# Eight one-hot buffers instead of four in the counting sweeps of a four-layer graph kernel

## The reference, cut to what matters

```
bias = bias.at[dst, src].set(edge_weight)          # layer 0: the last edge of a cell wins
agg = segment_sum(h[src] * norm, dst)              # layer 1
msg = h_all[src, edge_type]; agg = segment_sum(msg, dst)   # layer 2
```

## Time and profile before

| what | value |
|---|---|
| median of 3 runs | 592.63 us (592.21 to 593.97) |
| the profiled execution | 597.42 us |
| its span in the profile | 595.7 us |
| PE busy | 533.4 us, 90% of the span |
| DVE busy | 397.4 us, 67% |
| POOL busy | 280.2 us, 47% |
| ACT busy | 226.2 us, 38% |
| mean granted TensorE clock | 0.96 of full speed |

### The profile page before, as it was taken

One profiled execution on the slowest core, in us unless ns is written; L12 is line 12 of the kernel. 1 busy time (PEld: TensorE's weight loads), 2 busy tenths in 40 slices (PEclk: granted clock), 3 DMA queues, 4 the chain that ended last, 5 costly groups with the idle time before them and its releaser, 6 DMA issues.

```text
span 595.7 us, 7620 instructions
## 1 busy us (share of the span) xinstructions
PE 533.4 (90%) x2437; PEld 351.2 (59%) x2452; DVE 397.4 (67%) x939; ACT 226.2 (38%) x473; POOL 280.2 (47%) x271
## 2 busy tenths in 40 slices
PE   6999999978999999888999999959798997999690
PEld 2444444436865546656778888838576885555460
DVE  7987978889757778965658734572246527773736
ACT  3020610035237754573512332333424127774333
POOL 7566556567468775305514300456541735754000
PEclk8999999997999999998999999979999899999896
DMA  7940000000673100236526200156752751100001
GB/s 267 395 108 2 0 0 0 0 1 2 238 226 102 54 19 1 72 109 209 149 67 208 72 0 1 42 170 167 205 158 87 210 154 45 37 1 1 1 0 71
DMA packets 29913, 54.37 MB, mean 91 GB/s; under 512 B 4962, under 2 KB 6446, under 8 KB 29368
## 3 DMA queue, kind: packets, MB, share of 16 engines
q1 hardware_dynamic: 15964, 27.14, 14.8%
q0 software_dynamic: 11968, 19.96, 11.0%
q10 hardware_dynamic: 1948, 6.86, 3.2%
HBM read 51.78 MB, written 2.17 MB: 91 GB/s over the span
## 4 chain that ended last, share of the span: by engine, by line
PE 62%; DVE 16%; ACT 7%; POOL 6%; DMA 6%; issue 3%; ACTq 0%; DVEq 0%; POOLq 0%
PE bank L499 19%; PE bank L476 9%; PE bank L478 9%; PE bank L477 9%; DMA wh<-w 4%; PE bank L594 4%; POOL wl L346 4%; PE bank L578 3%; PE bank L569 3%; ACT gap L769 2%; PE bank L671 2%; DVE h L1044 2%; DVE h L1043 2%; PE bank L669 2%; PE bank L670 2%
## 5 line engine op out<-in xcount | busy, mean ns | idle before, releaser
L346 POOL TENSOR_TENSOR wl<-wraw,wh 128x512 fp32r<-128x512 f32 (+1 forms) x78 | 103.9, 1351 | 86.3 <-DMA wh<-w 21.0
L499 PE MATMUL bank<-hot 128*128 128x512 bf16 x529 | 118.6, 383 | 3.7 <-DVE hot L1092 2.9
L387 POOL DMA_INDIRECT edge_bias<-ewn,cell_at x68 | 75.0, 1103 | 43.7 <-DVE cell_at L1086 19.5
L499 PEld LDWEIGHTS bank<-hot 128*128 128x128 bf16 x544 | 53.5, 99 | 68.5 <-DVE hot L1092 3.4
L476 PE MATMUL bank<-wh,tl 128*128 128x512 f32 x176 | 71.4, 406 | 2.3 <-DVE tl L1003 2.3
L478 PE MATMUL bank<-wh,th 128*128 128x512 f32 x176 | 69.4, 394 | 0.0
L477 PE MATMUL bank<-wl,th 128*128 128x512 f32 x176 | 69.2, 393 | 0.0
L476 PE MATMUL bank<-th,wl 128*128 128x512 f32 x104 | 43.3, 417 | 10.0 <-DVE packed L1179 6.4
L477 PE MATMUL bank<-tl,wh 128*128 128x512 f32 x104 | 42.7, 410 | 0.0
L478 PE MATMUL bank<-th,wh 128*128 128x512 f32 x104 | 42.5, 409 | 0.0
L1091 DVE TENSOR_SCALAR hot<-iota,ef 128x512 bf16<-128x512 f16 x68 | 30.6, 450 | 16.1 <-PE bank L499 8.2
(11 more groups left out here) (188 smaller groups left out, 1023.6 us busy)
## 6 DMA issues: line engine op xcount, KB each, us to landing
wraw<-w SPq DMA_DIRECT2D x26, 256.0 KB
wh<-w POOLq DMA_DIRECT2D x6, 1024.0 KB, 6.2
keyb<-edge_keys ACTq DMA_DIRECT2D x4, 1088.0 KB, 11.1
wh<-w_rel POOLq DMA_DIRECT2D x4, 1024.0 KB, 5.8
wraw<-w_rel SPq DMA_DIRECT2D x16, 256.0 KB
wraw<-w_qkv SPq DMA_DIRECT2D x8, 256.0 KB
wraw<-w_o SPq DMA_DIRECT2D x8, 256.0 KB
wh<-w_o POOLq DMA_DIRECT2D x2, 1024.0 KB, 5.8
```

The costliest lines, as they stand in the source:

```text
L346: pool.tensor_tensor(wl[n % WSLOTS][:, k, 0:width], wraw[:, q % 3, 0:width], wh[n % WSLOTS][:, k, 0:width], ALU.subtract).then_inc(s["w_lo ...
L387: pool.indirect_dma_start(out=bias_dram, out_offset=bass.IndirectOffsetOnAxis(ap=cell_at[:, c:c + 1], axis=0), in_=ewn[:, c:c + 1], in_off ...
L499: mm = pe.matmul(ps(name)[:], hot[:, slot, 0, i * P:(i + 1) * P], hot[:, slot, 1 + kind, :], start=False, stop=last, skip_group_check=True)
```

## The change

Four more buffers, `hot_late`, are laid over the memory of `wl[1]` and `wl[2]`, so that `RING` is 8. DVE may then build eight chunks before PE has used the first of them. The sweeps are counted in chunks (`SWEEPS` = 32 and 36), and PE's loops and DVE's loop of the first sweep run over eight chunks. On DVE, the first four chunks of the second sweep are all built before banks 4 to 7 are copied (three before), its first group needs no wait on `hot_used2`, then a loop runs three times over two groups, and a last group stands alone. The lag of placing is eight chunks as before. Since `wl[1]` and `wl[2]` are now also one-hot buffers, DVE waits ahead of L1173, and POOL ahead of `low(2)`, until PE has used 32 chunks of the second sweep.

```diff
@@ -37,10 +37,9 @@
-RING = 4
-TBLOCKS = CHUNKS // RING
-CBLOCKS = (8, 9)
-FIRST_PLACED = 2
+RING = 8
+SWEEPS = (32, 36)
+BEHIND = 2 * GROUP
...
@@ -49,9 +48,9 @@
-assert E == CHUNKS * P and sum(CBLOCKS) == TBLOCKS and max(CBLOCKS) * RING * P <= 2 * MIDDLE < BASE
+assert E == CHUNKS * P and sum(SWEEPS) == CHUNKS and max(SWEEPS) * P <= 2 * MIDDLE < BASE
-assert RING == GROUP and CBLOCKS[1] == 9
+assert RING == 2 * GROUP == BEHIND and SWEEPS[0] % RING == 0 and SWEEPS[1] % RING == GROUP
 
 
 WEIGHTS = ([("w0_q", K, D), ("w0_k", K, D), ("w0_v", K, D), ("w0_o", K, D), ("w0_1", K, D), ("w1", K, D), ("w2_self", K, D)]
@@ -183,7 +182,8 @@
         deg = sb("deg", [P, 6, T], F32)
         ones = sb("ones", [P, P], F32R)
         wh = [sb(f"wh{s}", [P, K, D], F32R) for s in range(WSLOTS)]
-        wl = [sb(f"wl{s}", [P, K, D], F32R) for s in range(WSLOTS)]
+        lows = region([("hot_late", [P, RING // 2, 3, N], BF16)], [(f"wl{s}", [P, K, D], F32R) for s in range(1, WSLOTS)])
+        wl = [sb("wl0", [P, K, D], F32R)] + [lows[f"wl{s}"] for s in range(1, WSLOTS)]
         wraw = sb("wraw", [P, 3, D], F32)
         nbias = sb("nbias", [P, T, N], F32)
         xh = region([("keyb", [P, E + (WINDOW - 1) * P], F32)],
@@ -205,7 +205,7 @@
...
-        cc = region([("hot", [P, RING, 3, N], BF16), ("packed", [P, 8, N], F32), ("later", [P, WINDOW * P], F16), ("eq", [P, GROUP, WINDOW * P], F16)],
+        cc = region([("hot", [P, RING // 2, 3, N], BF16), ("packed", [P, 8, N], F32), ("later", [P, WINDOW * P], F16), ("eq", [P, GROUP, WINDOW * P], F16)],
...
@@ -217,6 +217,7 @@
         sp = [ab["sp"][:, n, :] for n in range(4)] + [rel_rows, deg_rows]
         rowh1, rowl1, rel_add, counth, countl = (ab[k] for k in ("rowh1", "rowl1", "rel_add", "counth", "countl"))
         hot, packed, call, call2, cph, cpl = (cc[k] for k in ("hot", "packed", "call", "call2", "cph", "cpl"))
+        hot = [hot[:, n] for n in range(RING // 2)] + [lows["hot_late"][:, n] for n in range(RING // 2)]
         later, eq = cc["later"], cc["eq"]
         ei, er, row_key = ab["ei"], ab["er"], ab["row_key"]
         msgh, msgl, hidh, hidl, probT = (cc[k] for k in ("msgh", "msgl", "hidh", "hidl", "probT"))
@@ -390,6 +391,7 @@
             for k in range(WINDOW):
                 pool.wait_ge(scattered[k], 16 * len(range(k, CHUNKS, WINDOW)))
             pool.dma_start(nbias[:], by_tile(bias_dram)).then_inc(s["bias_loaded"], 16)
+            pool.wait_ge(s["hot_used2"], SWEEPS[1] - GROUP)
             low(2)
             cast(3)
             low(3)
@@ -496,25 +498,25 @@
                 pe.wait_ge(s["hot_ready"], total_c)
                 for n, name in enumerate(names):
                     i, kind = n % T, n // T
-                    mm = pe.matmul(ps(name)[:], hot[:, slot, 0, i * P:(i + 1) * P], hot[:, slot, 1 + kind, :],
+                    mm = pe.matmul(ps(name)[:], hot[slot][:, 0, i * P:(i + 1) * P], hot[slot][:, 1 + kind, :],
                                    start=False, stop=last, skip_group_check=True)
                     if last:
                         finish(mm, name)
                 if not last:
                     mm.then_inc(s[f"hot_used{sweep}"], 1)
 
-            def sweep(w, blocks, before, names):
+            def sweep(w, count, before, names):
                 for name in names:
                     begin(name)
                     pe.matmul(ps(name)[:], minus[:], offset[:], start=True, stop=False, skip_group_check=True)
                 for slot in range(RING):
                     chunk(slot, before + slot + 1, w, slot, names, False)
-                with pe.Fori(1, blocks - 1) as b:
+                whole_rings = (count - 1) // RING
+                with pe.Fori(1, whole_rings) as b:
                     for slot in range(RING):
                         chunk(None, b * RING + (before + slot + 1), w, slot, names, False)
-                for slot in range(RING):
-                    c = (blocks - 1) * RING + slot
-                    chunk(c, before + c + 1, w, slot, names, slot == RING - 1)
+                for c in range(whole_rings * RING, count):
+                    chunk(c, before + c + 1, w, c % RING, names, c == count - 1)
 
             def columns(name, w, ready, ks=K, n=K):
 
@@ -600,8 +602,8 @@
             pe.wait_ge(s["centre_set"], 3)
             before = 0
             for c in range(2):
-                sweep(1 + c, CBLOCKS[c], before, [("counts", c, b) for b in range(8)])
-                before += CBLOCKS[c] * RING
+                sweep(1 + c, SWEEPS[c], before, [("counts", c, b) for b in range(8)])
+                before += SWEEPS[c]
             columns("q0", 0, lambda i: pe.wait_ge(s["x_low"], K))
             columns("k0", 1, lambda i: pe.wait_ge(s["k_low"], K))
             rows("v0", 2, lambda i: None)
@@ -1088,23 +1090,24 @@
 
             def build_chunk(j, slot):
 
-                dve.tensor_scalar(hot[:, slot, 0, :], iota[:, 0:N], ef[:, 0, bass.ds(j, 1)], None, ALU.is_equal)
-                dve.tensor_scalar(hot[:, slot, 1:3, :].rearrange("p a n -> p (a n)"), iota[:], pair_dst[:, bass.ds(j, 1)],
+                dve.tensor_scalar(hot[slot][:, 0, :], iota[:, 0:N], ef[:, 0, bass.ds(j, 1)], None, ALU.is_equal)
+                dve.tensor_scalar(hot[slot][:, 1:3, :].rearrange("p a n -> p (a n)"), iota[:], pair_dst[:, bass.ds(j, 1)],
                                   digit[:, bass.ds(j, 1)], ALU.is_equal, ALU.mult).then_inc(s["hot_ready"], 1)
 
-            def build_and_place(sweep, at, first, c, group):
-
-                for slot in range(RING - 1):
-                    dve.wait_ge(s[f"hot_used{sweep}"], at + (slot - RING + 1))
-                    build_chunk(at + (first + slot), slot)
-                    mark(c, slot)
-                mark(c, RING - 1)
-                dve.wait_ge(s[f"hot_used{sweep}"], at)
-                build_chunk(at + (first + RING - 1), RING - 1)
+            def build_and_place(sweep, at, first, slots, c, group):
+
+                for n in range(GROUP):
+                    if n == GROUP - 1:
+                        mark(c, n)
+                    if sweep:
+                        dve.wait_ge(s[f"hot_used{sweep}"], at + (n - RING + 1))
+                    build_chunk(at + (first + n), slots + n)
+                    if n < GROUP - 1:
+                        mark(c, n)
                 settle(c, group)
 
             dve.wait_ge(s["ld_iota"], 16)
-            for slot in range(RING):
+            for slot in range(GROUP):
                 build_chunk(slot, slot)
             for n, value in enumerate((EPS, ROUND, -ROUND)):
                 link(dve.memset(const[:, n:n + 1], value))
@@ -1113,27 +1116,25 @@
             link(dve.memset(keyb[:, E:], -1.0))
             dve.wait_ge(s["ld_ew"], 16)
             link(dve.tensor_scalar(ewn[:], ew[:], 8.0, None, ALU.mult))
-            for block in range(1, FIRST_PLACED):
-                for slot in range(RING):
-                    j = block * RING + slot
-                    dve.wait_ge(s["hot_used1"], j - RING + 1)
-                    build_chunk(j, slot)
+            for slot in range(GROUP, RING):
+                build_chunk(slot, slot)
             dve.wait_ge(s["ld_later"], 16)
             dve.wait_ge(ld_keys[0], 16)
             dve.wait_ge(ld_keys[1], 16)
-            with dve.Fori(FIRST_PLACED, CBLOCKS[0]) as b:
-                build_and_place(1, b * RING, 0, b * RING + (-FIRST_PLACED * RING), b + (-FIRST_PLACED))
-
-            before, behind = CBLOCKS[0] * RING, (CBLOCKS[0] - FIRST_PLACED) * RING
+            with dve.Fori(1, SWEEPS[0] // RING) as b:
+                for half in range(2):
+                    at = b * RING + half * GROUP
+                    build_and_place(1, at, 0, half * GROUP, at + (-BEHIND), b * 2 + (half - BEHIND // GROUP))
+
+            before, behind = SWEEPS[0], SWEEPS[0] - BEHIND
             dve.wait_ge(ld_keys[2], 16)
             dve.wait_ge(ld_keys[3], 16)
-            for slot in range(RING - 1):
+            for slot in range(GROUP):
                 dve.wait_ge(s["hot_used1"], before - RING + slot + 1)
                 build_chunk(before + slot, slot)
             for i in range(T):
                 wait_full(dve, ("counts", 0, 4 + i))
                 frees(dve.tensor_copy(packed[:, 4 + i, :], ps(("counts", 0, 4 + i))[:]), ("counts", 0, 4 + i))
-            build_chunk(before + RING - 1, RING - 1)
             for k in range(GROUP):
                 mark(behind, k)
             settle(behind, behind // GROUP)
@@ -1145,12 +1146,18 @@
                                          in1=packed[:, 4 * pair:4 * pair + 4, :][:, tile, :], op0=ALU.mult, op1=ALU.add)\
                     .then_inc(s["unpacked"], 1)
 
-            with dve.Fori(0, (CBLOCKS[1] - 1) // 2) as g:
-                for odd in range(2):
-                    at = g * (2 * RING) + (1 + odd) * RING
-                    build_and_place(2, at, before, at + behind, g * 2 + (1 + odd + behind // GROUP))
```

(15 more changed lines are left out.)

## The result

The changed kernel takes 600.88 us (597.15 to 604.31), the kernel before 593.37 beside it: ratio 1.0125, 95% interval 1.0077 to 1.0173. It is **slower**, by a little over 1% and clear of the noise, where I forecast 586.7 with 0.86 for faster. Its profiled execution took 600.26, against the 597.42 of before.

A forecast was written before the change was run, and what follows sets the result against it. PE bounds the sweeps; DVE's late tail then idles PE ahead of `q0` and halves its clock. Gain 5.65 + 2.4 = 8.05, less 2.1 for a late semaphore in the profile only: 592.63 - 5.9 = 586.7 us, range 584.0 to 590.1.

The forecast's parts named there:

- in the sweeps PE never waits for a buffer: Sweeps: DVE waits for PE (8.2 us in 13 waits), at no cost; more buffers can't shorten the sweeps themselves.
- Loops and slots: Sweeps: PE's loop body doubles, the back edge is passed fewer times; cost taken as 0.
- is the kind of thing that only the profiled execution may have: Ahead of `q0`: the semaphore 2.4 late is absent from timed runs, taking 2.1 us off the gain.
- 5.65 + 2.4 = 8.05: Up to the end of `q0`: 5.65 us from less idle plus 2.4 us from the clock, against the profiled execution.
- the forecast was for 5.9: Whole kernel, timed runs: gain of 8.05 - 2.1 = 5.9 us, giving 586.7; chance 0.50.
- Idle: 0.8 forecast: PE ahead of `q0`: 0.8 us of idle instead of 6.45, a gain of 5.65 us.
- The tail: DVE's marks and L1173 at the sweeps' end: L1173 done between 126.1 and 127.7, beside the sweep ending at 129.75.
- Idle of the kernel before without the late semaphore: PE ahead of `q0` in the kernel before, timed runs: 4.35 us, still enough for the clock to fall.
- The clock: First 12 matmuls of `q0`: full clock instead of half, 2.4 us gained, bounds 0 to 3.4.
- POOL: Scatters get faster: last one ends at 134 to 138.4 instead of 146.52; `low(2)` at 144 to 148.5, covered.
- Behind the attention's start everything hangs on PE: From the attention's start to the end: all work shifts earlier by the whole gain.
- (d): Sweeps: DVE without pauses slows POOL's scatters from 1.42 to 1.96 each; 8.7 us slower, 601.3; chance 0.03.

The follow-up runs named there:

- b_again: The kernel before, unchanged, run again beside the changed kernel for a second profile; median 592.33 us.
- chip C: The chip of the third group of experiments: changed kernel as it is, with PE's loops written out, with DVE's written out, and the kernel before.
- a_third: The changed kernel as it is, run once more beside the kernel before; ratio 1.0101 (1.0058 to 1.0144).
- a_again: The changed kernel as it is, run again beside the kernel before; ratio 0.9892 (0.9815 to 0.9968).
- a_pe_unrolled: The changed kernel with PE's sweep loops written out; ratio to the kernel before 0.9869 (0.9821 to 0.9918).
- chip F: The chip where the changed kernel ran with its first 20 scatters up to three in flight and the other 48 one at a time.
- a_lag4: The changed kernel with eight buffers, but each build waits for the chunk four back; ratio to the kernel before 1.0057 (1.0027 to 1.0087).
- a_scatter_split: The changed kernel with 20 scatters beside the first sweep and the other 48 held until behind the second; read for the sweeps, no total time given.
- a_scatter_two: The changed kernel with at most two scatters in flight instead of three; ratio to the kernel before 0.9943 (0.9898 to 0.9988).

## Why the prediction was wrong, and what of it was right

**The step that failed:** "in the sweeps PE never waits for a buffer. It is DVE that waits for PE ..., and that costs nothing while it lasts", and with it "Loops and slots ... I take 0". PE's gaps in the sweeps (5.8), the half clock (1.7) and the ends at the gaps (1.5) cost 9.0 us where I had 0. I had two signs and argued one away. Beside DVE's 8.2 us in 13 waits, which I read as DVE being early, the same view of the kernel before has a line that I passed over:

```profile
DVE hot L1091 <- remote: 5.9, 2, 3.1
```

In b_again, where nothing stops, DVE waits more in all (12.2 in 26), but never over 1.1 at a time: an early DVE shows as many short waits, a late release as a few long ones. And of the 32nd chunk's release, 2.4 late, I wrote that it "is the kind of thing that only the profiled execution may have". It was a symptom of a fault that also sits in the timed runs: on chip C a_third took 603.29 as a median and 603.31 with the profile, the kernel before 597.66 and 597.86.

**Sum for the first measurement.** I had 5.65 + 2.4 = 8.05 gained up to the end of `q0`. The trace has 6.45 - 0.90 = 5.55 of it, but 9.0 lost ahead: `q0` starts 3.4 later (139.64 against 136.20). The scores start only 1.0 later (172.48 against 171.45): the 2.4 of the clock are there, to the tenth. The rest of the 2.8 between the spans lies behind. The medians are 7.5 apart (600.88 against 593.37), and what the other 4.7 are these two profiles can't say: that of before is of an execution 4.8 slower than the median of its first three. On chip C they can: there the scores start 177.6 - 172.2 = 5.4 later, and the medians are 5.6 apart.

**Where nothing stops**, the forecast was for 5.9, and the steps up to the attention hold one by one. Idle: 0.8 forecast, 0.89 found. The tail: L1173 (now L1181) done 2.1 to 3.6 ahead of the sweeps' end, 3.2 found. Idle of the kernel before without the late semaphore: 4.35 forecast, 4.48, 4.39 and 4.48 found. The clock: b_again has half clock behind its idle of 4.48 (0.62 over 135.50:142.00, 1.00 in a_again).

```profile
135.50:142.00 6.50, 6.49 (x18) 5.21 (x19) 6.50 (x12) 4.23 (x6) 5.58 (x4) 0.62 0.03 3
```

```profile
131.20:138.00 6.80, 6.75 (x30) 5.63 (x31) 6.80 (x12) 6.64 (x11) 4.18 (x5) 1.00 0.01 0
```

POOL: the last scatter forecast for 134 to 138.4, found at 136.2. `q0` starts 135.51 - 131.25 = 4.3 earlier and the scores 170.66 - 164.07 = 6.6 earlier. 0.7 of each is that this execution's sweeps end at 130.35 and not at 131.03, by no doing of the change; the other 5.9 of the scores are what I forecast.

**What was mis-sized even there:** "Behind the attention's start everything hangs on PE ..., so I let all of it shift". From the scores' start to the end b_again takes 420.3 and a_again 425.3:

```profile
170.66:591.00 420.34, 373.58 (x1749) 267.14 (x1748) 254.34 (x582) 187.37 (x412) 176.40 (x172) 0.96 0.30 91
```

```profile
164.07:589.40 425.33, 376.65 (x1749) 268.88 (x1748) 254.48 (x582) 187.42 (x412) 174.60 (x170) 0.95 0.30 88
```

Five of the 6.6 are given back. Of these, PE's one wait for `wl` of POOL (L347, 3.8 against 1.6 for L346) is 2.2, and PE is busy 3.1 longer with the same 1749 matmuls, at a lower mean clock. a_pe_unrolled, with its scores at 163.2, keeps it: 419.8. So this varies from execution to execution by as much as the gain. The medians differ by 3.3 (588.99 against 592.33), somewhat more than half of what I forecast, but a_again has 4 runs and its interval allows 1.9 to 11 us, so they don't settle the size.

**The rivals.** None named this. (d) had the right sign and the right partner, POOL's scatters, with the wrong victim: it priced scatters slowed by DVE, where PE's releases and issue are held up while scatters run. That it named POOL's scatters was luck. Scatters of the changed kernel are not slow: 39 start between 72 and 130 us in a_again, 35 in b_again, 33 both before and after where there are stops. The rule of the Trainium skill that I set beside it (SBUF — State Buffer, "Who interferes with whom", descriptors of GpSimd starved by VectorE) would show as late scatters; the trace has denser ones, so that rule did not decide here.

**What stays open.** By which path a scatter holds up PE: landings, descriptors and POOL's own issue weren't told apart. Why chips differ, as A, B and D had no stops, C, E and F had. And what exactly makes stops worse with eight buffers: a release is acted on up to 3.5 us behind its matmul with four, up to 8.7 to 12.2 with eight (6.1 on chip F). The longer runs of scatters would explain it. With four buffers the bursts are of two or three releases and PE has no gap; with eight they are of three or four, and each stretch with gaps is followed within 2 us by one. Whether held releases are what stops PE's issue was not tried. a_lag4 would tell which part of the change does it, but it met a chip without stops.

## What to carry to other kernels

An engine that waits "for nothing that costs" should be asked whether it is early or its partner late: compare when the last instruction that uses the buffer ends with when the release is acted on. A release that is late by more than a chunk is a fault on the partner's side or on the signal's way, and a change that leans on prompt releases inherits it. A gain of 1% needs its comparison on more than one chip: here the same code was 1.0125 and 1.0101 in two measurements and 0.9892 in a third, whose interval lies wholly apart from the other two.

## What the hardware showed that I had not expected

A semaphore that a matmul signals can arrive up to 12 us after the matmul has ended (due at 49.8 and acted on at 62.0 in a_scatter_split, at 61.4 in the first profile of the changed kernel). Several then arrive 0.09 us apart, and PE may issue one matmul at a time meanwhile, with no wait of its own to show for it. It was seen only beside scatters of POOL at one every 1.3 us, it ended within 2.2 us of the last of a run of them, and it was seen only on some chips. In those profiles records of the scatters' semaphores are missing (386 to 561 of 1091 are there in the kernels whose scatters were left as they are), but a_scatter_two lacks some too and has no stop, so a thinned record is a sign to look further and no more. And gaps of 0.3 to 1.0 us between single matmuls cost the clock once (0.50 from 59.80 on) and once not: the stretch from 95 to 100 has as few matmuls, and stays at 1.00.

```profile
54.00:60.00 6.00, 2.59 (x10) 0.65 (x9) 1.35 (x4) 0.00 (x0) 4.14 (x5) 0.98 0.02 0
95.00:100.00 5.00, 2.60 (x11) 0.82 (x10) 1.83 (x6) 0.00 (x0) 2.52 (x3) 1.00 0.01 0
```
